# Gathered unit rows in a ring of 16, ten units instead of twelve summed by one-hots, result gathers without waits for TensorE

## The reference

```python
x = x + xattn(layernorm(x), ctx_512, ...)     # 2 x 256 rows of 256, 16 heads
x = x + ffn(layernorm(x), ...)
# ffn: T = 512 tokens, E = 32 experts, TOP_K = 4 (from 2 of 4 groups), MOE_I = 128
combine = zeros((T, E)).at[arange(T)[:, None], topk_idx].add(topk_w)
def body(acc, packed):
    w1e, w3e, w2e, ce = packed
    return acc + ce[:, None] * swiglu(x, w1e, w3e, w2e), None
routed, _ = lax.scan(body, zeros_like(x), (w1, w3, w2, combine.T))
return routed + swiglu(x, ws1, ws3, ws2)
```

## Time and profile before

| | |
|---|---|
| median of 3 runs | 312.37 us (311.81 to 312.76) |
| span of the profiled execution, first to last instruction | 310.6 us |
| the median less that span | 1.8 us |
| TensorE busy | 291.4 us, 94% of the span |
| VectorE, ScalarE, GpSimd busy | 60%, 51%, 43% |
| granted TensorE clock, mean | 0.986 of full |

### The profile page before, as it was taken

How to read it: one execution, slowest core, us unless ns; L and a number is a source line. 1 busy time by engine, 2 the same in 40 slices (tenths; PEclk the granted TensorE clock), 3 DMA queues, 4 the chain that set the end, 5 groups by cost and what they waited for, 6 DMA issues and landing times.

```text
span 310.6 us, 5507 instructions
## 1 busy us (share of the span) xinstructions
PE 291.4 (94%) x1856; PEld 207.2 (67%) x1856; DVE 185.6 (60%) x432; ACT 157.7 (51%) x374; POOL 132.9 (43%) x123
## 2 busy tenths in 40 slices
PE   8898899999999999999999999987799999999981
PEld 6665768765777666786668777655457666676661
DVE  4595776657867687766753555178862223342775
ACT  3535877667676766777671455391013333332420
POOL 0662928784017680079930000000165554456571
PEclk9999999999999999999999999999689999999998
DMA  7950007000700001600059964220032554433233
GB/s 233 397 190 1 0 1 239 33 0 2 270 5 0 0 3 28 228 0 3 0 161 395 402 262 154 86 68 0 0 100 72 160 155 146 152 103 81 70 86 106
DMA packets 15850, 34.10 MB, mean 110 GB/s; under 512 B 2512, under 2 KB 8400, under 8 KB 15824
## 3 DMA queue, kind: packets, MB, share of 16 engines
q1 hardware_dynamic: 13520, 27.46, 24.7%
q0 software_dynamic: 2304, 6.29, 7.2%
HBM read 30.07 MB, written 3.67 MB: 109 GB/s over the span
## 4 chain that ended last, share of the span: by engine, by line
PE 85%; DVE 7%; ACT 2%; issue 2%; POOL 2%; DMA 1%; POOLq 0%; DVEq 0%; ACTq 0%
PE bank L564 10%; PE bank L547 9%; PE bank L656 9%; PE bank L538 6%; PE bank L539 5%; PE bank L518 5%; PE bank L677 4%; PE bank L433 4%; PE bank L435 3%; PE bank L434 3%; PE bank L462 3%; PE bank L493 3%; PE bank L496 3%; PE bank L645 3%; PE bank L440 2%; PE bank L633 2%
## 5 line engine op out<-in xcount | busy, mean ns | idle before, releaser
L1314 POOL DMA_INDIRECT rope<-xn_rows,idx x32 | 30.9, 965 | 88.8 <-DVE idx L1221 66.4
L339 POOL TENSOR_TENSOR rtmp<-abuf,rope 128x512 f32<-128x512 f32 x21 | 27.3, 1302 | 60.4 <-PE bank L435 41.1
L820 ACT ACTIVATE prob<-bank,nmax 128x512 f32<-128x512 f32 x48 | 32.7, 686 | 36.8 <-DVE nmax L996 36.8
L996 DVE TENSOR_REDUCE nmax<-bank 128x1 f32<-128x512 f32 x64 | 41.1, 685 | 6.6 <-PE bank L539 6.0
L656 PE MATMUL bank<-wall,nmat 128*64 (+1 forms) x256 | 31.2, 385 | 0.0
L564 PE MATMUL bank<-pT,kvr 128*64 128x256 f32 x256 | 31.2, 385 | 0.0
L1014 DVE COPY pT<-bank 128x512 f32<-128x512 f32 x32 | 22.0, 687 | 12.2 <-PE bank L547 11.8
L538 PE MATMUL bank<-kdup,qsp 128*128 128x512 f32 x64 | 28.4, 443 | 0.8 <-ACT prob L820 0.8
L968 DVE COPY abuf<-bank 64x512 f32<-64x512 f32 x24 | 16.4, 684 | 19.5 <-ACT abuf L796 19.1
L342 POOL TENSOR_TENSOR roped<-rtmp 128x512 f32<-128x512 f32 x21 | 27.2, 1296 | 1.6
L340 POOL TENSOR_TENSOR rtmp<-abuf,rope 128x512 f32<-128x512 f32 x21 | 27.4, 1305 | 0.0
(11 more groups left out here) (205 smaller groups left out, 561.8 us busy)
## 6 DMA issues: line engine op xcount, KB each, us to landing
wall<-in_w_exp SPq DMA_DIRECT2D x32, 384.0 KB, 7.6
wring<-in_w_attn SPq DMA_DIRECT2D x16, 224.0 KB, 4.0
wring<-in_w_attn SPq DMA_DIRECT2D x4, 640.0 KB, 8.1
y_rows<-nmat SPq DMA_DIRECT2D x10, 256.0 KB
wring<-in_w_attn SPq DMA_DIRECT2D x4, 512.0 KB, 7.0
rope<-in_rope_q SPq DMA_DIRECT2D x1, 768.0 KB, 6.8
x_sb<-in_x SPq DMA_DIRECT2D x1, 512.0 KB, 3.7
xn_rows<-xn SPq DMA_DIRECT2D x4, 128.0 KB, 1.7
```

The source lines that it names most:

```text
L339: eng.tensor_tensor(t0.rearrange("p (b s) -> p b s", b=B), own.rearrange("p (b s) -> p b s", b=B), cos, ALU.mult)
L820: act.activation(probs[t % 4], s_ps[t % 3][:, :], ACT.Exp, bias=nmax[:, t:t + 1], accum_out=psum_e[:, t:t + 1]).then_inc(s_exp, 1)
L996: dve.tensor_reduce(nmax[:, t:t + 1], s_ps[t % 3][:, :], AX.X, ALU.max, negate=True).then_inc(s_max, 1)
L1314: pool.indirect_dma_start(xg[:, u % XG, :], None, xn_dram, bass.IndirectOffsetOnAxis(idx[:, 1, u:u + 1], 0)) \
```

## The change

The ring for gathered rows has 16 places instead of 4 and lies in the buffer pT, which attention no longer needs, so that the first 16 gathers wait for nothing and gather u waits for the x_rows of unit u - 16. DIR is 10, so that 22 units are written and gathered and five pairs are summed by one-hots. The gates of collect are gone, and one wait for the products of slot_weights (sw_mm) stands in their place. The last combine has a function of its own, which finishes the first bank of PSUM before the second and signals each, and VectorE's last adds wait for one bank at a time.

```diff
--- before.py
+++ after.py
@@ -44,9 +44,9 @@
 NX = E + 1
 BLK = 64
 NU = E
-DIR = 12
+DIR = 10
 NG_U = NU - DIR
-XG, XS, YS, GS = 4, 4, 4, 4
+XG, XS, YS, GS = 16, 4, 4, 4
 NK = TT * TOPK
 C_LT, C_ONE, C_IOTA, C_PAD, C_VAL, C_TS, C_TI, C_END = 0, P, P + E, P + E + BLK, P + 2 * E + BLK, P + 2 * E + BLK + NK, \
     P + 3 * E + BLK + NK, P + 4 * E + BLK + NK
@@ -211,7 +211,7 @@
         one_both = ones[:, 0:2 * T].rearrange("p (s i e) -> p s i e", s=2, e=E)
         one_r = ones[:, 2 * T:4 * T].rearrange("p (i r) -> p i r", r=BLK)
         sel_a, sel_b, em_a = ct_flat[:, 4 * T:5 * T], ct_flat[:, 5 * T:6 * T], ct_flat[:, 6 * T:6 * T + T // 2]
-        xg = rope[:, :, :, :].rearrange("p k a s -> p (k a) s")
+        xg = pT[:, :, :, :].rearrange("p r c s -> p (r c) s")
         xTu = nmat[:, 0:XS, :].rearrange("p r (d q) -> p r d q", d=ND)
         yu = nmat[:, XS:XS + YS, :]
         kv_flat = kv[:, :, :].rearrange("p n c -> p (n c)")
@@ -273,7 +273,7 @@
         gt_mm = sem("gt_mm"); gt_ev = sem("gt_ev"); yu_mm = sem("yu_mm"); yu_ev = sem("yu_ev")
         fill_in = sem("fill_in"); q_own = sem("q_own"); q_swap = sem("q_swap")
         d_iota = sem("d_iota"); w_one = sem("w_one"); sw_mm = sem("sw_mm"); sw_done = sem("sw_done")
-        oh_done = sem("oh_done"); yd_hi = sem("yd_hi"); acc_mm = sem("acc_mm")
+        acc_end = sem("acc_end"); oh_done = sem("oh_done"); yd_hi = sem("yd_hi"); acc_mm = sem("acc_mm")
         fin = sem("fin")
 
 
@@ -632,9 +632,20 @@
                         for tt in range(TT):
                             mm = pe.matmul(acc_ps[tt // 2][:, (tt % 2) * D:(tt % 2 + 1) * D],
                                            one_hot[:, p % 2, i, tt * P:(tt + 1) * P], yd[:, p % 2, i, hl, :],
-                                           start=(p == 0 and i == 0 and hl == 0 and tt % 2 == 0),
-                                           stop=(p == DIR // 2 - 1 and i == 1 and hl == 1 and tt % 2 == 1), skip_group_check=True)
+                                           start=(p == 0 and i == 0 and hl == 0 and tt % 2 == 0), stop=False, skip_group_check=True)
                 mm.then_inc(acc_mm, 1)
+
+            def combine_last(p):
+                pe.wait_ge(yu_ev, NG_U // 2 + p + 1)
+                pe.wait_ge(oh_done, p + 1)
+                for tt in range(TT):
+                    for i in range(2):
+                        for hl in range(2):
+                            mm = pe.matmul(acc_ps[tt // 2][:, (tt % 2) * D:(tt % 2 + 1) * D],
+                                           one_hot[:, p % 2, i, tt * P:(tt + 1) * P], yd[:, p % 2, i, hl, :],
+                                           start=False, stop=(i == 1 and hl == 1 and tt % 2 == 1), skip_group_check=True)
+                    if tt % 2 == 1:
+                        mm.then_inc(acc_end, 1)
 
             def x_rows(j):
                 if j >= 1:
@@ -760,7 +771,9 @@
                     hidden(j - 1)
                 if j == NU // 2 + 1:
                     out_rows(j - 2)
-                if j - 3 >= NG_U // 2:
+                if j == NU // 2 + 2:
+                    combine_last(DIR // 2 - 1)
+                elif j - 3 >= NG_U // 2:
                     combine(j - 3 - NG_U // 2)
                 if 2 <= j < NU // 2 + 1:
                     out_rows(j - 2)
@@ -1267,8 +1280,8 @@
                     p = j - 4 - NG_U // 2
                     add_rows(PACE * p, PACE * (p + 1))
             add_rows(PACE * (DIR // 2 - 2), NK)
-            dve.wait_ge(acc_mm, DIR // 2)
             for tt in range(TT):
+                dve.wait_ge(acc_end, tt // 2 + 1)
                 dve.tensor_tensor(x_sb[:, tt, :], acc_ps[tt // 2][:, (tt % 2) * D:(tt % 2 + 1) * D], x_sb[:, tt, :], ALU.add) \
                    .then_inc(fin, 1)
 
@@ -1322,19 +1335,13 @@
             for tt in range(TT):
                 pool.wait_ge(d_xn[tt], 16)
             pool.wait_ge(idx_done, 1)
-            for u in range(XG):
-                gather(u)
-            for u in range(XG, NU):
+            for u in range(NU):
                 gather(u)
             pool.wait_ge(placed, 1)
             for r in range(YS // 2):
-                pool.wait_ge(d_yu[r], 16 * (NG_U // YS))
-            G2 = NG_U // 2
-            gates = {0: (acc_mm, 1), 1: (yu_mm, G2 + 2), 3: (hu_mm, G2 + 4), 5: (yu_mm, G2 + 3), 6: (hu_mm, G2 + 5), 8: (yu_mm, G2 + 4),
-                     9: (hu_mm, G2 + 6), 11: (yu_mm, G2 + 5)}
+                pool.wait_ge(d_yu[r], 16 * len(range(r, NG_U // 2, YS // 2)))
+            pool.wait_ge(sw_mm, 1)
             for i in range(NK):
-                if i in gates:
-                    pool.wait_ge(*gates[i])
                 collect(*divmod(i, TOPK))
 
 
```

## The result

The changed kernel takes 342.56 us (median of 4 runs, 342.14 to 343.47), the kernel before 312.56 us beside it (311.81 to 313.07). The ratio is 1.0975, with a 95% interval of 1.0948 to 1.1001: 30 us slower, where 1.8 us faster was forecast. Rival A of the prediction, TensorE's signals held while gathers run without a pause, in its lasting form, had 340 us and a chance of 0.09. It is the nearest to what came.

What follows compares the result with a forecast made beforehand. Three engines (TensorE, VectorE, GpSimd) reach the end within 2.2 us of each other. The last adds start at 304.7, VectorE-bound, instead of 306.50: 1.8 us off the 310.6 span gives 308.8, plus 1.8 carried over, 310.6 us; range 309.0 to 317.2.

Steps and rivals of the forecast that it cites:

- Rival A: Gathers without a pause hold TensorE's signals; lasting form: 15 us at unit rows, about 14 at results, 340 us, chance 0.09.
- part 1: Ring of 16: GpSimd's 32 unit row gathers end at 264.2 instead of 277.55; worth 0 to TensorE.
- part 3: Result gathers without gates: 15 steps of 1.25 us, last landed at 300.5, 5.4 us earlier than 305.89.
- two signs: Rival A's evidence: ScalarE, VectorE, GpSimd released together 1.3 us after a fifth gather; ScalarE released 1.1 us after the first burst.
- Rival A's milder form: Stalls of 2.2 us come back, two or three of them on the path: 315.0 to 317.2 us, chance 0.14.
- rival B: No change: one stall of 2.2 us among the ungated result gathers makes TensorE wait, 312.8 us, chance 0.14.
- Rival C: VectorE stretches GpSimd's queue: each result gather costs 1.6 us, not 1.25; 312.3 us, chance 0.05.
- the rule: VectorE operations taking both ports block GpSimd's descriptor writes; factor five on two gathers would lose 5 us, trace shows 0.03 to 0.04 each.
- parts 2 and 4: Tail: one combine fewer, VectorE's last weighted rows 2.6 us earlier, then ten adds of 5.3 us; VectorE last at 304.7, gain 1.8.
- bank by bank end of combine_last: Stop-by-half ordering of the last combine: gives nothing while VectorE is last, otherwise at most 1.05 us.
- The first gather of results: Starts at 278.9 (before: 280.04): eleventh pair's rows at 276.3, plus 2.5 for the write and 0.1.

Runs made afterwards that it cites:

- e1_ring: The kernel before with the ring of 16 alone (12 one-hot units, gates kept), on a chip without holds: 312.4 us.
- e2_gates: The kernel before with only the gates on the result gathers removed (ring of 4), on a chip without holds: 311.12 us.
- e3_paced_x: The changed kernel with its ring of 16 used as one of four, so unit row gathers wait for x_rows again: 310.8 us.
- m1 to m4: The changed kernel with unit row gathers paused by GpSimd, of quarter rows, plain transfers from GpSimd, or plain from SyncE: 313.1, 309.17, 310.13, 310.36 us.
- n1: The changed kernel with ten unit row gathers unpaused, GpSimd's own pauses from then on, and result gathers of a quarter of the data: 309.87 us.
- e5_again: The changed kernel run again unchanged, five executions: 343.4 us, ratio 1.0998 to the kernel before.
- first group's chip: Chip where ring alone, gates gone alone, paced ring and GpSimd's own pauses in both stretches ran: 312.4, 311.12, 310.8, 312.72 us, beside 311.95 before.
- e9_ring: The kernel before with the ring of 16 alone, same program as e1_ring, on another chip, one with holds: 330.5 us.

## Why the prediction was wrong

- **The step that failed is part 1, "Running ahead gives TensorE nothing: 0", together with part 3, which priced 16 gathers without gates as 15 x 1.25 us of GpSimd's time and as nothing for TensorE.** Both took the gathers to touch TensorE only through semaphores and data. On a holding chip the first costs 18.6 us alone and the second 16.6.
- **Rival A had the nearest mechanism, and the size.** It forecast 15 + 14 us; 17.7 + 14.8 were measured. The 18 gathers and the end of the first stretch at 246.7 were 20 and 249.12, since x_rows(1)'s signal still got through at 237.7. What it lacked is that TensorE's instructions crawl and not only its signals, and that this goes with the chip. Its weight, 0.09, was too low: half of the eight comparisons had holds.
- **Of its two signs one was real.** At 287.28 to 287.60 three engines are released within 0.32 us, which is not scatter of one of them. The same place in e1_ring, with the same gates on a chip without holds, has ScalarE waiting 2.73 us and not 3.98, VectorE 1.25 and not 3.43, GpSimd 0.30 and not 1.59, and TensorE's gap of 0.52 us is not there. The other sign, ScalarE's release at 232.90, is none: the transposes have their end by the record at 232.64, and e2_gates, with the same ring of four on a chip without holds, has the same wait. First e1_ring, then e2_gates, both on their timelines of ScalarE:

```profile
286.39 0.84 ACT L913 ACTIVATE xnT<-bank,wslot 128x256 fp32r<-128x256 f32 x2 [2.73 <-PE bank L677]
```

```profile
232.60 0.59 ACT L890 COPY nmat<-bank 128x512 f32<-128x512 f32 x1 [3.19 <-PE bank L645]
```

- **Rival A's milder form and rival B** would have needed holds of 2.2 us that end by themselves. The measured ones last until some 3 us after the stretch (249.12 to 252.76 is 3.6; 316.83 to 319.73 is 2.9).
- **Rival C and the rule** (VectorE keeps GpSimd from writing descriptors): the sixteen gathers of the changed kernel average 961 ns, before 984. Neither way is there anything of a factor of five; the rule does not show here, and no run tells whether VectorE's operations in this part are of the kind that it names.
- **The tail, parts 2 and 4, held where nothing was held up.** e3_paced_x has the changed kernel's tail on a chip without holds. Its VectorE, to be read beside the earlier trace rows:

```profile
298.75 0.88 DVE L1214 SCALAR_TENSOR_TENSOR xnT<-bank,wslot,xnT 128x256 fp32r<-128x256 f32 x2
299.54 5.16 DVE L1223 SCALAR_TENSOR_TENSOR x_sb<-ctT,topw,x_sb 128x256 f32<-128x256 f32 x10
304.74 1.42 DVE L1285 TENSOR_TENSOR x_sb<-bank,x_sb 128x256 f32<-128x256 f32 x4
```

  Weighted rows at 298.75 (forecast 298.6), ten adds of 5.16 us in one block without a wait (5.3), the four last adds at 304.74 (304.7), 310.8 us in all (310.6). That the times agree to a few hundredths is in part luck, since x_rows(3) was at 240.00 there and at 239.65 in the trace forecast from: between the two 65.05 us were forecast and 64.74 measured, so the tail was 0.3 us better than forecast. The changed kernel has the same block of ten, 5.16 us, only from 331.68 on. Against the kernel before on the same chip that is 1.15 us less in single runs, 0.4%, near what a measurement can tell. The changed kernel itself never ran on a chip without holds; its time there, near 310.8, is read off the kernels that share its tail. In the changed kernel VectorE was last, not TensorE, and the bank by bank end of combine_last was hidden, as said.
- **The first gather of results** was forecast at 278.9 and came at 280.20 in e3_paced_x. Counted from x_rows(3) it is 0.95 us late there (40.20 for 39.25), and 0.3 to 0.6 in m1 to m4 and n1: the way from the eleventh pair to the first gather was taken that much too short. It cost nothing, since every gather had landed when its add came.
- **What was wrong beside the sum** is that the forecast took one trace for the kernel. Its late release at 287.3 belonged to the chip that it was taken on. On a chip of the other kind the same forecast would have come out right, with the same step unsupported; that would have been luck.

What stays open: what makes a chip hold TensorE. Four of eight comparisons had holds and four had none. The seven whose chips are known were on seven chips, so that it is a lasting mark of a chip and not of its state at the time is argued, not shown; within a comparison it never changed (the five executions of e5_again lie within 2 us). Open too is what in a gather does it, now that the amount of data is excluded for the result gathers: GpSimd's part in it, the 128 separate rows, or the completion.

## What to carry to other kernels

GpSimd's gathers can hold TensorE though the instructions held wait for no gather. Where several engines are released at the same moment, shortly after another one paused, treat it as a mechanism and price it by the length of the new stretch. Waits that pace a queue of gathers by TensorE's progress, and a small ring, look like waste in a profile (16.9 us of idle, and nothing gained from it in the chain); here they are worth 30 us on some chips and cost about 1 us on others. Before a change removes pacing, run both kernels on more than one chip: on the first group's chip alone, no part of this change loses anything measurable.

## What the runs showed of the hardware

- In four comparisons of eight, each but the first on a chip known to differ, GpSimd gathers of 128 rows at one per 1.25 us slowed TensorE after the first few gathers: transposes that take 0.66 us for four came one in 1.40 us (the changed kernel) or one in 0.70 to 1.43 (e9_ring), with nothing to wait for. Its later signals came only 2.9 to 3.6 us after the stretch had ended. VectorE, ScalarE and GpSimd kept their own speed: an eviction took 0.58 us and a gather 0.95 in the hole as outside. In the other four nothing was held, with 32 such gathers in a row in e1_ring.
- For the result gathers the hold was the same for rows of 256 B (one run) and of 1 KB (four).
- Two gathers in 3.55 us never held it in the traces kept; two in 3.15 us, behind ten without a pause, let it recover only over some 20 us (one run).
- The Trainium skill, "SBUF — State Buffer", section "SBUF: two separate sides", says of SBUF's engine ports that "PE, ACT, and DVE's dedicated pair never wait on anyone". The trace does not contradict the sentence on ports, since it does not show where TensorE stood, but it shows TensorE held beside GpSimd's gathers, for most of 17.7 us; whoever reads the sentence as "TensorE can't be slowed by them" would be wrong here.
